# Row factors of attention pairs 3 to 15 sent as rows through memory, with idle products from the start and a new order of all steps

## The chip, the cores and the metric

The kernel runs on one core of one Trainium2 chip. The metric is device microseconds for one execution of the whole program: the lower the better. The core has five engines with a queue of instructions each: TensorE (PE in the profile, its weight loads PEld), VectorE (DVE), ScalarE (ACT), GpSimd (POOL) and SyncE (SP), which here only issues DMAs. Every engine takes its own instructions strictly in order and waits on semaphores that other engines or DMAs raise.

## The reference

32 graphs of 256 nodes with 128 features each pass four layers; each layer is added to its input and normalized over the features.

```python
# layers 0 and 1: graph attention
h = x @ W.T
z = (h @ a_src)[:, :, None] + (h @ a_dst)[:, None, :]
alpha = softmax(where(adj == 0, -big, leaky_relu(z, 0.2)))
x = layernorm(x + alpha @ h)
# layer 2: gated scores; adj is 0 or 1 here
alpha = sigmoid(where(adj == 1, leaky((x * a0) @ x.T), -big))
x = layernorm(x + alpha @ x + bias2)
# layer 3: relation 1 only
x = layernorm(x + (adj == 1) @ x @ W3[0] + bias3)
```

## The kernel before, in words

The graphs go in 16 pairs, n = 0 to 15 (H = 2 graphs a pair). A step, as `weight0:5`, is one stage of one layer for one pair; `ORDER` lists, for each of the five engines, the steps in the order in which that engine takes them, written out by hand. `counts` turns the lists into semaphore values, so that a step waits until the steps it reads from are done. `BANKS` says which of the eight 2 KB PSUM banks each PE step of each pair writes; `bank_free` makes PE wait until the former holder of the bank was read.

In an attention layer a pair passes these steps. PE projects (`h`, line 1097): besides the 128 features each node gets two logits, which VectorE copies out (`logits`, lines 811 and 813). Softmax of a leaky sum factors: apart from a factor that cancels in the normalization, the weight of node j for node i is the larger of a factor of i and a factor of j, times j's value factor, where the edge exists. ScalarE takes the exponentials of the logits (`gains`, line 609: 128 x 8). The factor of j is a column in SBUF, one number in each partition. The factor of i is wanted as a row, the same 256 numbers in all 128 partitions. `rows` (line 1114) makes it on PE: four transposes for a pair, each of a column of `gain` broadcast to 128 columns, into a PSUM bank. `weight` (line 837) is then four VectorE instructions for a pair: larger of row (from PSUM) and column, times the mask. PE multiplies the weights with the values (`out`, line 1157). Beside this path `dT` (line 1103) transposes the other logit into 4 rows for the largest (`peak`, `top`, `dmax`), from which the values' exponent is offset.

Layer 2 goes `xT`, `xTa`, `score` (line 1124), `sigmoid`, `umax`, `alpha`, `out2`; layer 3 `high`, `low`, `agg` (line 1134), `out3` (line 1154). Statistics (`stats`, line 888), residuals (`res`, lines 868 and 880) and small steps on VectorE, powers (`pow`, line 535), bias sums (`bias`, line 530), scaled copies (`xTa`, line 559), low parts (`low`, line 541) and some normalizations (line 549) on GpSimd stand between them.

GpSimd issues the mask loads, at most `AHEAD` = 6 pairs ahead of `weight0`. SP issues the loads of x, as rows (`x`) and turned (`xT`), and the stores. PE begins with five products of zeros (`idle_products`, line 1165) after the waits for the identity matrix, which GpSimd makes after its memset of `zero`.

Of the kernel before, what the change touches and what calls it, by code (L numbers as in the profile page):

```python
# [1287 lines left out]
```

## Time and profile before

| what | value |
|---|---|
| median of 3 runs (lowest to highest) | 253.18 us (252.33 to 253.56) |
| the profiled execution | 254.48 us |
| span of that execution | 251.4 us |
| PE busy | 227.2 us (90%) |
| VectorE busy | 229.2 us (91%) |
| ScalarE, GpSimd busy | 189.8 us (75%), 173.4 us (69%) |
| mean granted TensorE clock | 0.982 of full speed |

The profile is of one execution. The span runs from the first instruction of the program to the last; 3.1 us of the execution lie around it. Busy time is the time in which at least one instruction of an engine runs. Successive VectorE or PE instructions overlap by some tens of nanoseconds, so a mean duration of one is longer than the step from one to the next: 16 products of line 1157 take 1.79 us in the chain, 0.11 us each, where one lasts 0.277 us. A product of 32-bit numbers is two records in the trace, a transpose is one. The chain is followed back from the last instruction, at each step to what released it.

### The profile page before, as it was taken

Reading aid. Unit: us, or ns where it says so; the run is one execution under the profiler, and the core shown is the slowest. Engines: PE = TensorE matmul, PEld = TensorE weight load, DVE = VectorE, ACT = ScalarE, POOL = GpSimd, SP = SyncE. Lnnn points to the kernel's source line nnn. Section 1 sums busy time; section 2 is a strip of 40 time slices with the busy share of each in tenths; the row PEclk is TensorE's granted clock in tenths of the full one; section 3 lists DMA queues with packets and bytes.
Section 4 is the critical chain, followed back from the end, with each engine's and each line's share of the span. In section 5 each row is a group of like instructions: output and inputs, shape, how many; then the busy total and the mean of one; then the engine's idle time right before and its main releaser. Section 6 shows DMA issues by size and latency. Waiting matters only on the chain.

```text
span 251.4 us, 5755 instructions
## 1 busy us (share of the span) xinstructions
PE 227.2 (90%) x1745; PEld 206.6 (82%) x1745; DVE 229.2 (91%) x812; ACT 189.8 (75%) x587; POOL 173.4 (69%) x260
## 2 busy tenths in 40 slices
PE   4998899999999999999999998999999979897850
PEld 4896788987999998988898997989989968776840
DVE  0399989998999999999999999999999888999894
ACT  2497856988968998867998956996891966977752
POOL 6032049878756786789837529984797996699982
PEclk9999999999999999999999999999999979999995
DMA  6999124501452313212230300011000110100106
GB/s 180 252 262 240 52 83 86 126 4 42 83 127 39 88 18 94 104 20 68 54 116 10 117 1 33 14 42 44 1 0 3 42 44 1 43 0 3 42 1 214
DMA packets 12144, 17.56 MB, mean 70 GB/s; under 512 B 1104, under 2 KB 5968, under 8 KB 12112
## 3 DMA queue, kind: packets, MB, share of 16 engines
q1 hardware_dynamic: 9520, 12.85, 16.4%
q0 software_dynamic: 2304, 4.20, 9.9%
q8 instruction: 15, 0.25, 0.4%
q10 hardware_dynamic: 288, 0.14, 0.2%
q14 instruction: 17, 0.14, 0.2%
HBM read 17.17 MB, written 4.19 MB: 85 GB/s over the span
## 4 chain that ended last, share of the span: by engine, by line
PE 55%; DVE 33%; DMA 5%; issue 3%; ACT 2%; POOL 1%; DVEq 0%; SPq 0%; POOLq 0%
PE banks L1157 25%; PE banks L1097 8%; DVE wgt_all L837 7%; PE banks L1124 6%; DVE fstats L888 6%; DMA w<-in_L_gnn_weight 5%; PE banks L1082 4%; DVE fres_all L880 4%; DVE fres_all L868 3%; PE banks L1154 3%; DVE banks L802 3%; PE banks L1114 3%; DVE wgt_all L845 2%; PE banks L1134 2%; PE banks L1107 1%
## 5 line engine op out<-in xcount | busy, mean ns | idle before, releaser
L535 POOL TENSOR_TENSOR frstd<-fvar,minus_half 128x4 f32<-128x4 f32 x64 | 64.8, 1018 | 23.3 <-ACT fvar L674 15.5
L1157 PE MATMUL banks<-vals_all,wgt_all 128*128 128x129 f32 x512 | 63.5, 277 | 3.6 <-ACT vals_all L625 1.9
L1157 PEld LDWEIGHTS banks<-vals_all,wgt_all 128*128 128x128 f32 x512 | 59.6, 191 | 6.6 <-ACT vals_all L625 3.1
L837 DVE SCALAR_TENSOR_TENSOR wgt_all<-banks,gain,mask_all 128x256 f32<-128x256 f32 x128 | 52.6, 471 | 0.3 <-PE banks L1114 0.2
L530 POOL TENSOR_TENSOR xb_all<-xs_all,bias_cen 128x256 f32<-128x256 f32 x62 | 44.5, 737 | 9.5 <-ACT xs_all L668 4.4
L888 DVE BATCH_NORM_STATS2 fstats<-fres_all 128x6 f32<-128x256 f32 x128 | 47.5, 414 | 0.1
L668 ACT ACTIVATE xs_all<-fres_all,frstd 128x128 f32<-128x128 f32 x112 | 35.7, 409 | 0.7 <-POOL frstd L535 0.6
L1157 PE MATMUL banks<-xs_all,wgt_all 128*128 128x128 f32 x256 | 32.7, 283 | 2.6 <-DVE wgt_all L845 2.5
L1157 PEld LDWEIGHTS banks<-xs_all,wgt_all 128*128 128x128 f32 x256 | 30.7, 196 | 3.8 <-DVE wgt_all L845 3.7
L1124 PE MATMUL banks<-fxT,fxTa 128*128 128x256 f32 x128 | 30.3, 381 | 0.0
L605 ACT COPY fxT<-banks 128x256 f32<-128x256 f32 x64 | 20.3, 382 | 12.7 <-PE banks L1082 12.7
L1124 PEld LDWEIGHTS banks<-fxT,fxTa 128*128 128x128 f32 x128 | 23.1, 190 | 2.7
L868 DVE SCALAR_TENSOR_TENSOR fres_all<-banks,xb_all 128x512 f32<-128x512 f32 x32 | 21.5, 679 | 3.5 <-PE banks L1157 2.1
L1114 PE MATMUL banks<-ident,gain 128*128 128x128 f32 x128 | 19.7, 279 | 1.6 <-ACT gain L609 1.2
L802 DVE TENSOR_TENSOR banks<-banks,wgt_all 128x512 f32<-128x512 f32 x32 | 20.9, 687 | 0.3
L641 ACT ACTIVATE wgt_all<-banks 128x512 f32<-128x512 f32 x32 | 19.3, 603 | 2.3 <-PE banks L1124 2.1
L541 POOL TENSOR_TENSOR fxTa<-xs_all,fxTa 128x256 f16<-128x256 f32 x28 | 18.2, 671 | 3.6 <-ACT fxTa L648 3.6
L845 DVE SCALAR_TENSOR_TENSOR wgt_all<-banks,mask_all 128x512 f32<-128x512 f32 x32 | 20.4, 678 | 0.0
L1134 PE MATMUL banks<-mask_all,fxTa 128*128 128x256 bf16 x128 | 16.8, 273 | 3.6 <-POOL fxTa L541 2.1
L1097 PE MATMUL banks<-w_fast,xT_all 128*128 128x130 f32 x128 | 19.4, 299 | 0.5 <-DVE w_fast L740 0.3
L625 ACT ACTIVATE vals_all<-banks,fscale 128x128 f32<-128x128 f32 x64 | 18.1, 377 | 2.0 <-POOL fscale L570 1.1
L642 ACT ACTIVATE banks<-banks 128x512 f32<-128x512 f32 x32 | 19.5, 609 | 0.0
(93 smaller groups left out, 419.2 us busy)
## 6 DMA issues: line engine op xcount, KB each, us to landing
xT_all<-x_turned SPq DMA_DIRECT2D x16, 256.0 KB, 2.9
mask_all<-adj_turned POOLq DMA_DIRECT2D x16, 256.0 KB, 6.0
x_all<-x_laid SPq DMA_DIRECT2D x16, 256.0 KB, 2.8
out<-xs_all SPq DMA_DIRECT2D x16, 256.0 KB, 2.2
bias<-biases_laid SPq DMA_DIRECT2D x1, 128.0 KB, 12.0
w_pack<-W_and_columns ACTq DMA_DIRECT2D x1, 68.0 KB, 3.2
w_fast<-W_turned ACTq DMA_DIRECT2D x1, 64.0 KB, 3.6
w_nat<-in_L_gnn_W SPq DMA_DIRECT2D x1, 64.0 KB, 8.3
```

The costliest lines, as they stand in the source:

```text
L530: nc.gpsimd.tensor_tensor(xb(u)[:, :, :], xs(u)[:, :, :], bias_cen[:, int(l) - 2, :, :], ALU.add).then_inc(fast_pool[k], 1)
L535: nc.gpsimd.tensor_tensor(frstd[:, int(l), slot(n), :], fvar[:, int(l), slot(n), :], minus_half[:, :, :], ALU.pow).then_inc(fast_pool[k], 1)
L668: last = nc.scalar.activation(xs(u)[:, b, :], fres(u)[:, b, :], ACT.Copy, scale=frstd[:, int(l), u, b:b + 1])
L802: nc.vector.tensor_tensor(scored, scored, wgt(u), ALU.max).then_inc(fast_dve[k], 1)
L837: last = nc.vector.scalar_tensor_tensor(out=wgt(u)[:, c, :], in0=place(f"rows{l}", u), scalar=gain[:, u, c, 1:2], in1=maskT(u)[:, c, :], o ...
L845: nc.vector.scalar_tensor_tensor(out=wgt(u), in0=scored, scalar=1.0, in1=maskT(u), op0=ALU.add, op1=ALU.mult).then_inc(fast_dve[k], 1)
L868: nc.vector.scalar_tensor_tensor(out=fres_all[:, pair(n, FRES), :, :], in0=gathered, scalar={"2": 0.5, "3": 1.0}[l], in1=xb_all[:, pair(n, ...
L888: nc.vector.bn_stats(fstats[:, u, :, :].rearrange("p b k -> p (b k)"), fres(u)[:, :, :].rearrange("p b d -> p d b")).then_inc(fast_dve[k], 1)
L1097: last = nc.tensor.matmul(place(f"h{l}", u)[:, b * HC:(b + 1) * HC], (xT_in if l == "0" else fxT)(u)[:, b * P:(b + 1) * P], w_fast[:, int( ...
L1114: last = nc.tensor.transpose(place(f"rows{l}", u)[:, b * P:(b + 1) * P], gain[:, u, b, 0:1].to_broadcast([P, P]), ident[:, :])
L1124: last = nc.tensor.matmul(place("score", u)[:, c * N:(c + 1) * N], fxTa(u)[:, c * P:(c + 1) * P], fxT(u)[:, :], start=True, stop=True)
L1157: last = nc.tensor.matmul(place(f"out{l}", u)[:, b * width:(b + 1) * width], wgt(u)[:, c, b * P:(b + 1) * P], (vals if l in "01" else xs)( ...
```

## The change

Row factors of pairs 0 to 2 stay as they are, in both layers. For pairs 3 to 15:

- `dT` transposes both logits of the pair, into two PSUM banks, instead of one.
- ScalarE takes the exponential of the turned logit (`rowx`, 4 x 128 from PSUM, into a small tile in SBUF; two such tiles for each layer).
- SP sends the tile as one row of 512 numbers to memory (`rowa`, 2 KB) and, when that has landed, loads the row into all 128 partitions (`rows`, 256 KB; `ROWS` = 3 buffers for each layer).
- `weight` reads the row from SBUF, and waits for `gains` and for that load. The PE step `rows` is gone for these pairs.

Besides: `AHEAD` is 3. The first four loads of `x` wait for `h0` of their pair. VectorE makes `zero`; PE's waits for the identity stand behind the idle products, which are seven. At five places in its list PE gets `warm` steps: a wait for the bank of the step behind, and then 5, 11, 5, 3 and 10 products of zeros into it. All five lists and `BANKS` are written anew. Three bias sums and one low part more stand on VectorE, one normalization of layer 1 fewer.

```diff
-AHEAD = 6
+AHEAD = 3
+ROWS, ROW_OUT = 3, 2
...
-    "rows0": "4 5 3 7 2 3 1 1 7 0 3 1 3 1 4 5",
+    "rows0": "4 4 4 - - - - - - - - - - - - -",
...
+SPREAD = {l: [n for name, layer, n in order("sp") if name + layer == "rows" + l] for l in "01"}
...
+        rows_all = sb("rows_all", [P, 2, ROWS, H * N])
+        row_all = sb("row_all", [H * NB, 2, ROW_OUT, P])
...
             def load_x(l, n, k):
                 if n >= X_IN:
                     sp.wait_ge(fast_dve[(n - X_IN) % K], at("dve", "res0", final(n - X_IN)))
+                else:
+                    sp.wait_ge(fast_pe[n], at("pe", "h0", final(n)))
...
+            def send_row(l, n, k):
+                q = SPREAD[l].index(n)
+                sp.wait_ge(fast_act[k], at("act", f"rowx{l}", n * H))
+                sp.dma_start(row_scratch[int(l), n].rearrange("(a d) -> a d", d=P), row_tile(l, n)).then_inc(fast_row_out[int(l)][q % ROW_OUT], 16)
+
+            def spread_rows(l, n, k):
+                q = SPREAD[l].index(n)
+                sp.wait_ge(fast_row_out[int(l)][q % ROW_OUT], 16 * (q // ROW_OUT) + 16)
+                if q >= ROWS:
+                    m = SPREAD[l][q - ROWS]
+                    sp.wait_ge(fast_dve[m % K], at("dve", f"weight{l}", final(m)))
+                sp.dma_start(rows_all[:, int(l), q % ROWS, :], row_scratch[int(l), n].rearrange("(a d) -> a d", a=1).to_broadcast([P, H * N])).then_inc(fast_rows_in[int(l)][q % ROWS], 16)
...
-            nc.gpsimd.memset(zero[:, :], 0.0).then_inc(zero_set, 1)
...
+            def exponential_rows(l, n, k):
+                q = SPREAD[l].index(n)
+                act.wait_ge(fast_pe[k], at("pe", f"dT{l}", n * H))
+                if q >= ROW_OUT:
+                    act.wait_ge(fast_row_out[int(l)][q % ROW_OUT], 16 * (q // ROW_OUT))
+                nc.scalar.activation(row_tile(l, n), place(f"h{l}", final(n))[0:H * NB, 260:260 + P], ACT.Exp, scale=SLOPE - 1).then_inc(fast_act[k], 1)
...
+            nc.vector.memset(zero[:, :], 0.0).then_inc(zero_set, 1)
...
             def weights(l, n, k):
-                dve.wait_ge(fast_pe[k], at("pe", f"rows{l}", final(n)))
+                spread = n in SPREAD[l]
+                if spread:
+                    q = SPREAD[l].index(n)
+                    dve.wait_ge(fast_act[k], at("act", f"gains{l}", n * H))
+                    dve.wait_ge(fast_rows_in[int(l)][q % ROWS], 16 * (q // ROWS) + 16)
+                else:
+                    dve.wait_ge(fast_pe[k], at("pe", f"rows{l}", final(n)))
...
-                        last = nc.vector.scalar_tensor_tensor(out=wgt(u)[:, c, :], in0=place(f"rows{l}", u), scalar=gain[:, u, c, 1:2],
+                        last = nc.vector.scalar_tensor_tensor(out=wgt(u)[:, c, :], in0=rows_in(l, u) if spread else place(f"rows{l}", u), scalar=gain[:, u, c, 1:2],
                                                               in1=maskT(u)[:, c, :], op0=ALU.max, op1=ALU.mult)
...
-            pe.wait_ge(ident_set, 2)
-            pe.wait_ge(ident_bf_set, 2)
...
             def gather_d(l, n, k):
                 pe.wait_ge(fast_dve[k], at("dve", f"logits{l}", n * H))
+                if n in SPREAD[l]:
+                    nc.tensor.transpose(place(f"h{l}", final(n))[0:H * NB, 260:260 + P], logit[:, int(l), slot(n), :, 0].rearrange("p u b -> p (u b)"), ident[:, :])
...
+            def keep_warm(count, phase, u):
+                bank_free(phase, u)
+                idle_products(count, bank_of(phase, u))
...
-            idle_products(5)
+            idle_products(7, 5)
             projection_columns()
-            for step, l, n in order("pe"):
-                steps[step](l, n, n % K)
+            pe.wait_ge(ident_set, 2)
+            pe.wait_ge(ident_bf_set, 2)
+            sequence = order("pe")
+            for q, (step, l, n) in enumerate(sequence):
+                if step == "warm":
+                    following, layer, m = sequence[q + 1]
+                    keep_warm(n, following + layer, m * H)
+                else:
+                    steps[step](l, n, n % K)
```

Where the lists move instructions is shown at three places, as the instructions stand in an engine's queue: line, operation, what is written and read, columns, count.

The beginning of PE's queue. Before, behind the waits for the identity: zeros, the product that gives the logits' columns, the projections of pairs 0 and 1, and then for each of these its logits' turn (`banks<-ident,logit`) and rows (`banks<-ident,gain`).

```order
L1165 MATMUL banks<-zero 128x128 x5
L1037 MATMUL banks<-w_pack 128x2
L1097 MATMUL banks<-w_fast,xT_all 128x130 x8
L1103 MATMUL banks<-ident,logit 4x128
L1114 MATMUL banks<-ident,gain 128x128 x4
L1103 MATMUL banks<-ident,logit 4x128
L1107 MATMUL banks<-ident,top 128x4 x2
L1114 MATMUL banks<-ident,gain 128x128 x4
L1157 MATMUL banks<-vals_all,wgt_all 128x129 x16
```

The same place now.

```order
L1210 MATMUL banks<-zero 128x128 x7
L1080 MATMUL banks<-w_pack 128x2
L1140 MATMUL banks<-w_fast,xT_all 128x130 x8
L1148 MATMUL banks<-ident,logit 4x128
L1159 MATMUL banks<-ident,gain 128x128 x4
L1086 MATMUL banks<-ident,w_cen 128x128
L1087 MATMUL banks<-w_pack,w_cen 128x2
L1148 MATMUL banks<-ident,logit 4x128
L1152 MATMUL banks<-ident,top 128x4
L1140 MATMUL banks<-w_fast,xT_all 128x130 x4
```

The turn of the second projection (`w_cen`) has come forward to between the rows of pairs 0 and 1, and the projection of pair 2 follows where the rows of pair 1 and the first outputs stood.

The middle of PE's queue, around pair 12 of layer 0 before: its logits' turn, an output of layer 1 for pair 9, its largest, its rows, an output of layer 2.

```order
L1103 MATMUL banks<-ident,logit 4x128
L1157 MATMUL banks<-vals_all,wgt_all 128x129 x8
L1107 MATMUL banks<-ident,top 128x4
L1114 MATMUL banks<-ident,gain 128x128 x4
L1157 MATMUL banks<-xs_all,wgt_all 128x128 x8
```

The same pair now; the rows in front are pair 13's two logit turns and a `warm` step.

```order
L1147 MATMUL banks<-ident,logit 4x128
L1148 MATMUL banks<-ident,logit 4x128
L1210 MATMUL banks<-zero 128x128 x5
L1125 MATMUL banks<-ident,xs_all 128x128 x4
L1202 MATMUL banks<-vals_all,wgt_all 128x129 x8
L1147 MATMUL banks<-ident,logit 4x128
L1148 MATMUL banks<-ident,logit 4x128
L1202 MATMUL banks<-vals_all,wgt_all 128x129 x8
L1152 MATMUL banks<-ident,top 128x4 x2
```

For the same pair the second transpose of the logits has come (line 1147), and the four transposes of `gain` behind the output are gone; the largest of pairs 12 and 13 stand together.

VectorE's queue ahead of the weights of layer 1, pair 3. Before: steps of layer 2 for pairs 0 and 1 (`res2`, statistics), logits and largest of other pairs, and then the weights of pair 6 (layer 0) and pair 3.

```order
L823 TENSOR_REDUCE minus_dmax<-banks 128x1
L845 SCALAR_TENSOR_TENSOR wgt_all<-banks,mask_all 128x512 x2
L868 SCALAR_TENSOR_TENSOR fres_all<-banks,xb_all 128x512
L813 TENSOR_TENSOR logit<-banks,frstd 128x4 x2
L888 BN_STATS fstats<-fres_all 128x6 x2
L868 SCALAR_TENSOR_TENSOR fres_all<-banks,xb_all 128x512
L819 TENSOR_REDUCE top<-banks 4x1
L888 BN_STATS fstats<-fres_all 128x6 x2
L811 COPY logit<-banks 128x4 x2
L823 TENSOR_REDUCE minus_dmax<-banks 128x1
L819 TENSOR_REDUCE top<-banks 4x1
L837 SCALAR_TENSOR_TENSOR wgt_all<-banks,gain,mask_all 128x256 x8
```

The same pair now. Its logits stand eight rows further up than the first row here; in between are one residual step (4 instructions) and one pair of statistics.

```order
L940 SCALAR_TENSOR_TENSOR fvar<-fstats,fvar 128x4
L851 COPY logit<-banks 128x4 x2
L859 TENSOR_REDUCE top<-banks 4x1
L853 TENSOR_TENSOR logit<-banks,frstd 128x4 x2
L859 TENSOR_REDUCE top<-banks 4x1
L863 TENSOR_REDUCE minus_dmax<-banks 128x1 x2
L859 TENSOR_REDUCE top<-banks 4x1
L948 SCALAR_TENSOR_TENSOR fcenter<-fstats,frstd 128x4
L863 TENSOR_REDUCE minus_dmax<-banks 128x1
L867 TENSOR_TENSOR fscale<-vals_all,frstd 128x4
L863 TENSOR_REDUCE minus_dmax<-banks 128x1
L883 SCALAR_TENSOR_TENSOR wgt_all<-rows_all,gain,mask_all 128x256 x4
```

The large operations of layer 2 are no longer between the logits and the weights of this pair, and the weights read `rows_all`, and so wait for the load, where they read a PSUM bank.

## Rows read from the trace of the kernel before

**Rows 1.** The windows: busy time of each engine in each stretch (first row: columns).
```profile
core 0: us, PE busy (x) PEld busy (x) DVE busy (x) ACT busy (x) POOL busy (x), PEclk, DMA share, GB/s
...
0.00:12.00 12.00, 8.46 (x40) 7.75 (x40) 2.40 (x14) 3.75 (x8) 4.28 (x13) 1.00 0.86 213
...
40.00:200.00 160.00, 156.88 (x1246) 144.65 (x1245) 156.57 (x557) 130.02 (x413) 119.67 (x176) 1.00 0.21 52
200.00:210.00 10.00, 8.19 (x52) 7.49 (x52) 7.60 (x26) 5.58 (x19) 7.61 (x12) 0.83 0.09 32
...
240.00:251.40 11.40, 2.35 (x18) 1.79 (x18) 7.25 (x24) 4.24 (x15) 6.47 (x8) 0.76 0.36 119
```

**Rows 2.** The chain that ended last, in 40 to 200 us, shares by line.
```profile
by line: PE banks L1157 32.8%; DVE wgt_all L837 10.1%; PE banks L1124 9.9%; PE banks L1097 8.9%; PE banks L1082 5.9%; PE banks L1114 4.5%; DVE fstats L888 3.8%; DVE fres_all L880 3.7%; PE banks L1154 3.6%; PE banks L1134 2.7%; issue 2.3%; P
```

**Rows 3.** The same chain in order of time: start, duration in us, what.
```profile
35.93 0.44 PE banks L1114 x4
```

**Rows 4.** Groups by line: count, busy us, mean ns of one, idle before.
```profile
L837 DVE SCALAR_TENSOR_TENSOR wgt_all<-banks,gain,mask_all 128x256 f32<-128x256 f32 x128 | 52.6, 471 | 0.3 <-PE banks L1114 0.2
...
L888 DVE BATCH_NORM_STATS2 fstats<-fres_all 128x6 f32<-128x256 f32 x128 | 47.5, 414 | 0.1
...
L541 POOL TENSOR_TENSOR fxTa<-xs_all,fxTa 128x256 f16<-128x256 f32 x28 | 18.2, 671 | 3.6 <-ACT fxTa L648 3.6
...
L625 ACT ACTIVATE vals_all<-banks,fscale 128x128 f32<-128x128 f32 x64 | 18.1, 377 | 2.0 <-POOL fscale L570 1.1 <-DVE fscale L827 0.8
...
L902 DVE SCALAR_TENSOR_TENSOR fcenter<-fstats,frstd 128x4 f32<-128x4 f32 x16 | 3.7, 231 | 0.0
...
L775 DVE TENSOR_TENSOR fxTa<-xs_all,fxTa 128x256 f16<-128x256 f32 x4 | 1.8, 476 | 0.0
...
L769 DVE TENSOR_TENSOR xb_all<-xs_all,bias_cen 128x256 f32<-128x256 f32 x2 | 0.7, 418 | 0.0
```

**Rows 5.** Timeline of PE, 2.8 to 18.5 us: start, duration, operation, idle before.
```profile
2.91 2.47 PE L1165 MATMUL banks<-zero 128*128 128x128 f32 x10 [2.91 <-DVE ones_col L723]
...
5.91 3.84 PE L1097 MATMUL banks<-w_fast,xT_all 128*128 128x130 f32 x16 [0.32 <-DVE w_fast L740]
...
17.29 1.06 PE L1097 MATMUL banks<-w_fast,xT_all 128*128 128x130 f32 x8
```

**Rows 6.** Timeline of VectorE, 112.5 to 117 us.
```profile
113.03 0.16 DVE L894 SCALAR_TENSOR_TENSOR fvar<-fstats,fvar 128x4 f32<-128x4 f32 x1
...
114.68 0.62 DVE L827 TENSOR_TENSOR fscale<-vals_all,frstd 128x4 f32<-128x4 f32 x1
...
115.36 0.62 DVE L902 SCALAR_TENSOR_TENSOR fcenter<-fstats,frstd 128x4 f32<-128x4 f32 x1
```

**Rows 7.** Timeline of GpSimd over the same time.
```profile
111.72 1.83 POOL L559 TENSOR_SCALAR fxTa<-fxT,w_pack 128x256 f32<-128x256 f32 x2 [0.39 <-PE banks L1114]
...
114.56 1.40 POOL L530 TENSOR_TENSOR xb_all<-xs_all,bias_cen 128x256 f32<-128x256 f32 x2
```

**Rows 8.** Line 902 by itself: count, shortest, median and longest duration in ns.
```profile
L902 DVE SCALAR_TENSOR_TENSOR fcenter<-fstats,frstd x16: 118/154/627, 36.6 to 222.3; 128x4 f32<-128x4 f32 x16
```

**Rows 9.** Line 530 of GpSimd in the same view.
```profile
L530 POOL TENSOR_TENSOR xb_all<-xs_all,bias_cen x62: 713/727/1302, 38.9 to 240.4; 128x256 f32<-128x256 f32 x62
```

**Rows 10.** DMA issues by line: count, KB each, median us to landing.
```profile
xT_all<-x_turned SPq DMA_DIRECT2D x16, 256.0 KB, 2.9
mask_all<-adj_turned POOLq DMA_DIRECT2D x16, 256.0 KB, 6.0
...
out<-xs_all SPq DMA_DIRECT2D x16, 256.0 KB, 2.2
```

**Rows 11.** The windows, 204 to 208 us; columns as in rows 1.
```profile
204.00:206.00 2.00, 1.90 (x12) 1.93 (x13) 2.00 (x5) 0.99 (x4) 2.00 (x4) 0.72 0.15 50
206.00:208.00 2.00, 2.00 (x12) 2.00 (x10) 0.99 (x3) 0.00 (x0) 2.00 (x4) 0.50 0.03 8
```

**Rows 12.** Timeline of PE, 202 to 208 us.
```profile
204.10 3.04 PE L1157 MATMUL banks<-xs_all,wgt_all 128*128 128x128 f32 x16 [0.64 <-DVE wgt_all L845]
```

More of the change, by code:

```diff
@@ L161 @@
 BANKS = {
[13 rows of a table removed]
[13 rows of a table added]
 }
-WHOLE = tuple(n + l for n in ("dT", "top", "gains", "v", "logits", "peak", "dmax", "rsum", "rinv", "var", "center", "pow") for l in "0123") + ("fscale", "seen", "res2", "res3")
+WHOLE = tuple(n + l for n in ("dT", "top", "gains", "rowx", "v", "logits", "peak", "dmax", "rsum", "rinv", "var", "center", "pow") for l in "0123") + ("fscale", "seen", "res2", "res3")
 PHASES = {"turn": 1, "h0": H, "rows0": 1, "out0": H, "xT1": 1, "h1": H, "rows1": 1, "out1": H,
@@ L216 @@
 UP_SQUARE = UP * UP
-COUNTS = {"pe": counts("pe", apart=("turn",)), "act": counts("act"), "dve": counts("dve", apart=("centre", "judge")), "pool": counts("pool", apart=("mask",))}
+COUNTS = {"pe": counts("pe", apart=("turn", "warm")), "act": counts("act"), "dve": counts("dve", apart=("centre", "judge")), "pool": counts("pool", apart=("mask",))}
 def at(engine, name, u):
@@ L255, with res_gnn_kernel @@
 HELD_BEFORE = holders()
-def res_gnn_kernel(nc, x, adj, W0, a_src0, a_dst0, W1, a1, a2_0, a2_1, a2_2, a2_3, bias2, adj3, W3, bias3, x_laid, x_turned, adj_turned, W0_turned, W0_and_columns, biases_laid, out):
+SPREAD = {l: [n for name, layer, n in order("sp") if name + layer == "rows" + l] for l in "01"}
+def res_gnn_kernel(nc, x, adj, W0, a_src0, a_dst0, W1, a1, a2_0, a2_1, a2_2, a2_3, bias2, adj3, W3, bias3, x_laid, x_turned, adj_turned, W0_turned, W0_and_columns, biases_laid, row_scratch, out):
     B, N, D = x.shape
@@ L333, in res_gnn_kernel @@
         wgt_all = sb("wgt_all", [P, WGT * H, NB, N])
-        sg_all = sb("sg_all", [P, SG * H, NB, N])
+        rows_all = sb("rows_all", [P, 2, ROWS, H * N])
+        row_all = sb("row_all", [H * NB, 2, ROW_OUT, P])
+        sg_all = rows_all[:, :, :, :].rearrange("p l q n -> p (l q n)")[:, 0:SG * H * NB * N].rearrange("p (q b n) -> p q b n", b=NB, n=N)
         logit = sb("logit", [P, 2, B, NB, 2])
@@ L373, in wgt, with rows_in, row_tile @@
             return wgt_all[:, u % (WGT * H), :, :]
+        def rows_in(l, u):
+            q = SPREAD[l].index(u // H) % ROWS
+            return rows_all[:, int(l), q, u % H * N:(u % H + 1) * N]
+        def row_tile(l, n):
+            return row_all[:, int(l), SPREAD[l].index(n) % ROW_OUT, :]
         def hi(u):
@@ L420, in res_gnn_kernel @@
         fast_pool = [sem(f"fast_pool_{k}") for k in range(K)]
+        fast_row_out = [[sem(f"fast_row_out_{l}{q}") for q in range(ROW_OUT)] for l in range(2)]
+        fast_rows_in = [[sem(f"fast_rows_in_{l}{q}") for q in range(ROWS)] for l in range(2)]
         fast_stored = [sem(f"fast_stored_{q}") for q in range(XS)]
@@ L477, in load_weights @@
                 sp.dma_start(dst, src).then_inc(signal, 16)
-            steps = {"weights": load_weights, "x": load_x, "xT": load_xT, "store": store}
+            steps = {"weights": load_weights, "x": load_x, "xT": load_xT, "rowa": send_row, "rows": spread_rows, "store": store}
             for step, l, n in order("sp"):
@@ L674, in variances @@
                 nc.scalar.activation(fvar[:, int(l), slot(n), :], fstats[:, slot(n), :, 2], ACT.Copy, bias=floor, scale=factor).then_inc(fast_act[k], 1)
-            steps = {"seen": note_odd, "var": variances, "xT": copy_xT, "gains": gains, "v": exponentials, "vals": values, "xTa": copy_xTa, "sigmoid": sigmoids,
+            steps = {"seen": note_odd, "var": variances, "xT": copy_xT, "gains": gains, "rowx": exponential_rows, "v": exponentials, "vals": values, "xTa": copy_xTa, "sigmoid": sigmoids,
                      "high": high_part, "agg": copy_gathered, "norm": normalize}
@@ L1162, in _, with idle_products @@
                      "score": scores, "agg": gather, "out": outputs, "turn": projection_turn}
-            def idle_products(count):
+            def idle_products(count, taken):
                 for _ in range(count):
-                    nc.tensor.matmul(banks[:, 5, 0:P], zero[:, :], zero[:, :], start=True, stop=True)
+                    nc.tensor.matmul(banks[:, taken, 0:P], zero[:, :], zero[:, :], start=True, stop=True)
+            def keep_warm(count, phase, u):
+                bank_free(phase, u)
+                idle_products(count, bank_of(phase, u))
             pe.wait_ge(zero_set, 1)
-            idle_products(5)
+            idle_products(7, 5)
             projection_columns()
-            for step, l, n in order("pe"):
-                steps[step](l, n, n % K)
+            pe.wait_ge(ident_set, 2)
[7 more added lines that the diff above has]
+                    steps[step](l, n, n % K)
             for n in range(TEAMS - K, TEAMS):
@@ L1283 @@
         args.append(nc.dram_tensor(name, a.shape, mybir.dt.from_np(a.dtype), kind="ExternalInput").ap())
+    args.append(nc.dram_tensor("row_scratch", (2, T, H * N), F32, kind="Internal").ap())
     args.append(nc.dram_tensor("out", (B, P, NB, D), F32, kind="ExternalOutput").ap())
```

197 rows, old and new, of tables (BANKS, ORDER) are left out of this document.

## The prediction

> **What bounds the kernel now.** I read the windows first, then the chain, then the groups by line, then timelines at the start, at a place where VectorE meets GpSimd, and at the tail. The windows show two engines at their limit at once: from 40 to 200 us PE is busy 156.88 of 160 us and VectorE 156.57 [rows 1]. Outside that stretch VectorE has its slack: 2.40 busy of the first 12 us, 7.60 of 200 to 210, 7.25 of the last 11.4. The chain of 40 to 200 us changes hands between both; PE's `rows` transposes (line 1114) are 4.5% of it, 7.2 us, and VectorE's weights (line 837) 10.1%, 16.2 us [rows 2]. The reader should see that a PE instruction taken away is worth at most what VectorE can follow: in that stretch VectorE waits only 160 - 156.57 = 3.4 us.
>
> The sum is made against the profiled execution, 254.48 us: span 251.4 and 3.1 around it. It is 1.3 above the median, 253.18; that is taken off at the end.
>
> **PE.** For 13 pairs in two layers four transposes go: 13 x 2 x 4 = 104. Four take 0.44 us, 0.11 each [rows 3]: 11.4 us. One transpose for each of the 26 comes, at the same 0.11: 2.9. The five `warm` steps hold 5 + 11 + 5 + 3 + 10 = 34 products of two records each, 68 x 0.11 = 7.5 us. They cost nothing where PE would wait for its next input anyway, and up to 7.5 where it would not. So PE loses between 8.5 and 1.0 us of work. Against VectorE's 3.4 us of waiting I take half: **-1.7**; ends 0 and -3.4.
>
> **VectorE.** 104 weights instructions read their row from SBUF instead of PSUM; the trace has none such. With a PSUM row one takes 471 ns [rows 4]. The nearest with 256 columns and two SBUF inputs are the bias sum, 418, and the low part, 476; with one SBUF input the statistics take 414 [rows 4]. The ends are 104 x -57 = -5.9 and 104 x +5 = +0.5. I take the bias sum, also 32 bit to 32 bit: 104 x -53 = -5.5. To VectorE come six bias instructions (6 x 0.42) and two low parts (2 x 0.48); four normalizations go, which I put at a bias sum each, and three small products come at 0.15 [rows 4, 8]: 2.5 + 1.0 - 1.7 + 0.5 = +2.3.
>
> Then the price of two SBUF inputs. At 114.68 and 115.36 us two VectorE instructions of four columns last 0.62 each [rows 6], while GpSimd is in its bias sums, 1.40 us for two [rows 7]. Both read two SBUF tensors. Line 902 alone lasts 154 in the median and 627 at the longest, mean 231 [rows 4, 8]: 77 ns lost for each instruction. At 113.03 a like instruction lasts 0.16 although GpSimd is in a scaled copy (line 559) [rows 6, 7]. So what holds VectorE up is GpSimd's instructions with two large inputs (lines 530 and 541), not all of its work. The weights now become such instructions. They come in 26 bursts of four; if only the first of a burst is exposed, 26 x 77 ns = 2.0 us, if each is, 104 x 77 ns = 8.0. GpSimd also yields: its line 530 has lasted 1302 instead of 727 [rows 9], which says that VectorE, once in, can keep going. I take +3.0, near the lower end for that reason. VectorE in sum: -5.5 + 2.3 + 3.0 = **-0.2**; ends -1.6 with 2.0 and -5.9, and +10.8 with 8.0 and +0.5.
>
> The page "SBUF — State Buffer" of the Trainium skill (section "Who interferes with whom") says that a VectorE instruction with two SBUF inputs contends with any GpSimd instruction that reads SBUF, and that the later one waits for the whole of the other. For the sums of lines 530 and 541 the trace agrees; for line 559 it does not [rows 6, 7]. By the page as it stands the loss would be larger than my +3.0; that is the second rival.
>
> **The way through memory.** From the logits to the weights a spread pair now needs: two transposes on PE with their lag, 0.4; the exponential, 128 columns from PSUM, like a value step 0.38 [rows 4]; the row to memory; the row back. The trace has neither DMA. The nearest to memory is a store, 2.2 us for 256 KB, the nearest back a load, 2.9 [rows 10]. The path is 0.4 + 0.38 + 2.2 + 2.9 = 5.9 us, without time in the queues of PE, ScalarE and SP; with 6.0 for the last DMA, as the masks have it [rows 10], it is 9.0. What covers it is VectorE's own work between logits and weights. I counted it in the new queue. For layer 1, pair 3 stand four residual instructions and two statistics (0.33 each, their 0.41 less the overlap) and some 22 small ones at about 0.08: 3.7 us. For pair 4 it is 4.7, for the other 24 at least 6.4, for 20 of them at least 7.0. So two are late for certain, by 2.2 and 1.2; behind the waiting weights stand all of VectorE's later steps, and PE's outputs wait for them. Part falls on waits that are there anyway: **+2.0**, ends 0 and +10.7 (a path of 7.5, which makes ten pairs late).
>
> SP is in order: while it waits for a row to land, loads of x and stores stand behind. Their data are wanted some steps later; nothing is counted. `AHEAD` = 3 lets a mask go only when the weights three pairs back are done; a mask lands in 6.0 in the median [rows 10], and between `weight0` of pairs three apart stands about that much of VectorE's work or more; nothing is counted either, and both are in the upper end.
>
> **The start.** PE's first product of zeros runs at 2.91, having waited for the identity [rows 5]. Now it waits for VectorE's memset alone, some 2 us earlier; two more products of 2 x 0.25 us each eat 1.0 of that. The projections of pairs 0 and 1 take 3.84 for 16 records, 0.24 each, and later 1.06 for 8 [rows 5]: the slow rate is the lower of PE's two clock levels as the steps show it, though the granted clock is 1.00 there. If PE is at its fast rate as much earlier as it begins, half of the 16 gain 0.11 each, 0.9. The column product, which all of it waits for, moves by at most 0.6. I take **-1.3**; ends 0 and -2.5.
>
> **The tail.** From 204 to 208 us the granted clock is 0.72 and then 0.50 [rows 11], after PE had been mostly waiting (8.19 busy of 200 to 210, [rows 1]). Sixteen products take 3.04 us [rows 12], where at 0.11 they take 1.8, and VectorE waits 2.4 us in those ten. A `warm` step of ten products now stands in this part of the program. I take 1.2 of clock and a third of the waits: **-2.0**; ends 0 and -3.6.
>
> **Sum.** -1.7 - 0.2 + 2.0 - 1.3 - 2.0 = -3.2: 254.48 - 3.2 = 251.3, less 1.3 for the median: 250.0.
>
> **Rivals.**
> 1. *PE is the bound and VectorE follows.* For: the chain is on PE for most of 40 to 200. Against: VectorE has 3.4 us to give. It would give the chain's 7.2, less half of the new transposes (1.4), 16.2 x 53/471 = 1.8 of the weights, 1.3 and 2.0 at the ends: -10.9, 242.3 us.
> 2. *The shared way into SBUF turns the weights slow* (slower). Place: every weights instruction while GpSimd is in lines 530 or 541. Those are 62 x 0.727 = 45.1 and 18.2 us [rows 4, 9], a quarter of the span; met there, an instruction waits half of 0.72. All 104 exposed: 104 x 0.25 x 0.36 = 9.4 in place of 3.0, +6.4, 256.4 us. It decides from a loss of about 6.2, where the sum is zero. If all of GpSimd's work held VectorE (119.67 of 160 us, [rows 1]), it would be 104 x 0.75 x 0.36 = 28 us, +25. Against: the undisturbed case above.
> 3. *The rows land late* (slower): a path of 7.5 makes ten pairs wait, 10.7 in place of 2.0: 258.7 us. For: three in-order queues lie on the path, and a load can stand behind another. Against: most gaps hold over 7 us.
> 4. *Nothing is gained in the middle or the tail*: VectorE sheds nothing, its waits only move. -1.3 - 0.2 + 2.0 = +0.5: 253.7 us. That the rows do leave PE, but to no effect, is this case.
>
> **How the numbers follow.** Forecast 0.45, with a range of its own from 246.5 to 252; rivals 0.10, 0.15, 0.15, 0.15. What a measurement here can tell from no change is about 0.5%, 1.27 us: faster is under 251.9, slower over 254.5. Faster: 0.42 of the forecast, all 0.10 of the first rival, 0.03 of the fourth: 0.55. Same: 0.02 of the forecast, 0.11 of the fourth, 0.04 of the second and third: 0.17. Slower: 0.28. The range that leaves out two in ten reaches from 243.5, by the first rival, to 257, between the second and the third.
>
> **What the profile would show.** Right: the weights at 0.42 with a few at 1.0; the first projection before 5.5 us; VectorE's waits for DMA only at two or three weights; 40 to 200 with PE busy some 6 us less and VectorE as before. Wrong: a mean of the weights over 0.50 (second rival), VectorE waiting for `rows_all` by more than 5 us (third), PE still busy 156 in that stretch with products of zeros, or VectorE's waits grown as PE's work fell.

## The result: slower by 7.5%, and the profile after

The changed kernel takes 271.81 us in the median of five (271.5 to 278.88), the kernel before 253.45 in the same set (252.33 to 253.6): a ratio of 1.0745 (95% interval 1.0714 to 1.0775, as in every bracket behind a ratio below), +18.4 us. A second set gave 1.0835 (1.0763 to 1.0906). The forecast was 250.0, faster; its range ended at 257. The rows of after come from a later profiled execution (span 270.8 us) whose time lies with the median; the first one took 278.88.

The windows, with the columns of [rows 1]:

```profile
0.00:12.00 12.00, 10.30 (x52) 9.81 (x53) 3.99 (x21) 5.52 (x10) 2.50 (x10) 1.00 0.89 234
12.00:40.00 28.00, 22.38 (x180) 19.66 (x179) 25.14 (x113) 18.12 (x62) 7.22 (x13) 1.00 0.67 169
40.00:200.00 160.00, 144.21 (x1110) 132.40 (x1109) 147.89 (x506) 120.30 (x385) 114.62 (x154) 0.97 0.31 84
200.00:210.00 10.00, 8.82 (x66) 7.57 (x64) 9.93 (x37) 8.39 (x29) 8.86 (x11) 1.00 0.25 81
```

In 40 to 200 us PE was busy 156.88 of 160 us and is now busy 144.21; VectorE went from 156.57 to 147.89. Both bounds have become loose at once: each waits 9 to 13 us more there, for the other engines. Then the groups by line that answer to [rows 4, 9], with GpSimd's small ones:

```profile
L883 DVE SCALAR_TENSOR_TENSOR wgt_all<-rows_all,gain,mask_all 128x256 f32<-128x256 f32 x104 | 48.2, 523 | 2.7 <-ACT vals_all L664 1.2 <-issue 0.9 <-DMA rows_all<-row_scratch 0.4
...
L567 POOL TENSOR_TENSOR frstd<-fvar,minus_half 128x4 f32<-128x4 f32 x64 | 67.5, 1061 | 13.4 <-DVE fvar L940 7.5 <-ACT fvar L713 3.3 <-DVE fvar L944 0.7
L562 POOL TENSOR_TENSOR xb_all<-xs_all,bias_cen 128x256 f32<-128x256 f32 x56 | 42.0, 768 | 12.8 <-ACT xs_all L704 8.0 <-ACT xs_all L707 4.7
...
L581 POOL TENSOR_SCALAR xs_all<-fres_all,frstd,fcenter 128x128 f32<-128x128 f32 x28 | 15.9, 578 | 1.2 <-DVE fcenter L948 1.1
...
L597 POOL TENSOR_SCALAR fvar<-fstats 128x4 f32<-128x4 f32 x25 | 8.3, 332 | 16.8 <-DVE fstats L934 16.4
```

The same views of single lines (shortest, median and longest ns, then first and last start):

```profile
L597 POOL TENSOR_SCALAR fvar<-fstats x25: 184/195/1934, 22.4 to 255.7; 128x4 f32<-128x4 f32 x25
...
L567 POOL TENSOR_TENSOR frstd<-fvar,minus_half x64: 996/1017/2614, 22.7 to 265.4; 128x4 f32<-128x4 f32 x64
...
L883 DVE SCALAR_TENSOR_TENSOR wgt_all<-rows_all,gain,mask_all x104: 456/477/1020, 25.9 to 233.4; 128x256 f32<-128x256 f32 x104
```

The weights are at 523 ns in the mean, above the 500 that the prediction named as the sign of its second rival. The surprise is on GpSimd: a variance of four columns that takes 0.195 us in the median lasts up to 1.934, a power of 1.017 up to 2.614. In before their longest were 0.37 and 1.08 us:

```profile
L565 POOL TENSOR_SCALAR fvar<-fstats x24: 193/197/367, 17.3 to 241.1; 128x4 f32<-128x4 f32 x24
...
L535 POOL TENSOR_TENSOR frstd<-fvar,minus_half x64: 997/1014/1078, 17.6 to 246.1; 128x4 f32<-128x4 f32 x64
```

Where that happens the timelines say why. VectorE, 82 to 97 us (start, duration, operation, idle before):

```profile
82.82 1.65 DVE L883 SCALAR_TENSOR_TENSOR wgt_all<-rows_all,gain,mask_all 128x256 f32<-128x256 f32 x4
84.41 0.27 DVE L859 TENSOR_REDUCE top<-banks 4x1 f32<-4x128 f32 x1
84.61 1.65 DVE L883 SCALAR_TENSOR_TENSOR wgt_all<-rows_all,gain,mask_all 128x256 f32<-128x256 f32 x4
86.19 0.21 DVE L863 TENSOR_REDUCE minus_dmax<-banks 128x1 f32<-128x4 f32 x2
87.19 0.16 DVE L948 SCALAR_TENSOR_TENSOR fcenter<-fstats,frstd 128x4 f32<-128x4 f32 x1 [0.79 <-POOL frstd L567]
...
89.73 3.49 DVE L883 SCALAR_TENSOR_TENSOR wgt_all<-rows_all,gain,mask_all 128x256 f32<-128x256 f32 x4
...
96.71 0.69 DVE L914 SCALAR_TENSOR_TENSOR fres_all<-banks,xb_all 128x512 f32<-128x512 f32 x1 [3.49 <-PE banks L1202]
```

GpSimd at the same time:

```profile
82.64 1.93 POOL L597 TENSOR_SCALAR fvar<-fstats 128x4 f32<-128x4 f32 x1
84.54 2.61 POOL L567 TENSOR_TENSOR frstd<-fvar,minus_half 128x4 f32<-128x4 f32 x1
...
89.72 1.59 POOL L562 TENSOR_TENSOR xb_all<-xs_all,bias_cen 128x256 f32<-128x256 f32 x2 [0.32 <-ACT xs_all L707]
91.28 1.66 POOL L573 TENSOR_TENSOR fxTa<-xs_all,fxTa 128x256 f16<-128x256 f32 x2
```

The variance ends when the first burst of four weights does, 84.57 against 84.47; the power behind it then loses the whole second burst, 2.61 - 1.02 = 1.6 us. VectorE itself waits 0.79 us for that power, and ScalarE's normalization 2.21. Five microseconds later it is the other way round: GpSimd's bias sums and low parts are under way, and four weights take 3.49 us instead of 1.65.

PE over the same time:

```profile
84.61 0.40 PE L1152 MATMUL banks<-ident,top 4*128 4x4 f32 x3
89.28 5.06 PE L1210 MATMUL banks<-zero 128*128 128x128 f32 x22 [4.27 <-DVE wgt_all L891]
94.13 2.14 PE L1202 MATMUL banks<-xs_all,wgt_all 128*128 128x128 f32 x13
```

PE waits 4.27 us for the gated weights (line 891), which have fallen behind, and only then do the products of zeros run, 5.06 us of them, ahead of outputs that need the same weights and could have started at 89.28. VectorE then waits 3.49 us, its longest wait of the whole run, for outputs that stand behind these zeros (its row at 96.71). The granted clock is already down by then:

```profile
88.00:90.00 2.00, 0.72 (x3) 0.73 (x4) 2.00 (x5) 1.13 (x4) 1.68 (x3) 0.60 0.77 129
90.00:92.00 2.00, 2.00 (x12) 2.00 (x10) 2.00 (x3) 1.97 (x8) 2.00 (x3) 0.50 0.81 133
```

### The profile page after: what moved, and what is told of

Its sections match the earlier page's. It is cut to its first block and busy times, and to the rows that moved or that the text cites. A ratio compares the mean times of both kernels' runs of the same rounds, so it can differ in the third digit from the quotient of the medians.

```text
span 277.1 us, 5858 instructions
## 1 busy us (share of the span) xinstructions
PE 237.2 (86%) x1739; PEld 214.6 (77%) x1739; DVE 238.4 (86%) x819; ACT 197.4 (71%) x617; POOL 180.4 (65%) x249
## 5 line engine op out<-in xcount | busy, mean ns | idle before, releaser
L567 POOL TENSOR_TENSOR frstd<-fvar,minus_half 128x4 f32<-128x4 f32 x64 | 67.7, 1064 | 14.7 <-DVE fvar L940 8.9
L1202 PE MATMUL banks<-vals_all,wgt_all 128*128 128x129 f32 x512 | 66.1, 284 | 4.0 <-DVE wgt_all L883 1.9
L1202 PEld LDWEIGHTS banks<-vals_all,wgt_all 128*128 128x128 f32 x512 | 63.2, 200 | 5.3 <-ACT vals_all L664 2.2
L883 DVE SCALAR_TENSOR_TENSOR wgt_all<-rows_all,gain,mask_all 128x256 f32<-128x256 f32 x104 | 48.9, 530 | 3.3 <-DMA rows_all<-row_scratch 3.3
L562 POOL TENSOR_TENSOR xb_all<-xs_all,bias_cen 128x256 f32<-128x256 f32 x56 | 41.3, 757 | 12.8 <-ACT xs_all L704 8.0
L546 POOL DMA_DIRECT2D mask_all<-adj_turned x16 | 9.6, 602 | 35.9 <-DVE wgt_all L883 26.7
L1210 PE MATMUL banks<-zero 128*128 128x128 f32 x82 | 15.6, 365 | 12.2 <-DVE wgt_all L891 8.3
L1210 PEld LDWEIGHTS banks<-zero 128*128 128x128 f32 x82 | 14.2, 268 | 13.4 <-DVE wgt_all L891 9.2
L842 DVE TENSOR_TENSOR banks<-banks,wgt_all 128x512 f32<-128x512 f32 x32 | 21.1, 692 | 3.5 <-ACT banks L681 3.5
L654 ACT ACTIVATE vals_all<-logit,minus_dmax 128x4 f32<-128x4 f32 x32 | 9.6, 301 | 16.6 <-DVE minus_dmax L863 12.3
L629 ACT ACTIVATE odd_square<-mask_all,minus_half 128x1024 bf16<-128x1024 bf16 x16 | 18.4, 1151 | 3.8 <-DMA mask_all<-adj_turned 3.7
```

What stands on the lines that cost most here:

```text
L562: nc.gpsimd.tensor_tensor(xb(u)[:, :, :], xs(u)[:, :, :], bias_cen[:, int(l) - 2, :, :], ALU.add).then_inc(fast_pool[k], 1)
L567: nc.gpsimd.tensor_tensor(frstd[:, int(l), slot(n), :], fvar[:, int(l), slot(n), :], minus_half[:, :, :], ALU.pow).then_inc(fast_pool[k], 1)
L842: nc.vector.tensor_tensor(scored, scored, wgt(u), ALU.max).then_inc(fast_dve[k], 1)
L883: last = nc.vector.scalar_tensor_tensor(out=wgt(u)[:, c, :], in0=rows_in(l, u) if spread else place(f"rows{l}", u), scalar=gain[:, u, c, 1:2],
L1202: last = nc.tensor.matmul(place(f"out{l}", u)[:, b * width:(b + 1) * width], wgt(u)[:, c, b * P:(b + 1) * P], (vals if l in "01" else xs)( ...
L1210: nc.tensor.matmul(banks[:, taken, 0:P], zero[:, :], zero[:, :], start=True, stop=True)
```

## The experiments

Three theories: A, weights with both inputs in SBUF and GpSimd hold each other up; B, something of the way through memory (late rows, SP's queue, `AHEAD`); C, the new order by itself, with the steps of zeros as its special case. Ratios are against runs of before in the same set.

**a0_again, a6_after.** The changed kernel unaltered.

> The changed kernel once more, for a second profile. Expected by every theory: 271.5 to 272.6 us, granted clock 0.97 to 0.98, and VectorE and PE both idle some 15 us more than before, in small pieces all over 12 to 120 us and 200 us to the end. If VectorE's idle time sits instead in one or two long waits, the theory that the new order as a whole is looser falls at once.

> The changed kernel itself, timed beside the next three on one chip. Expected by every theory: 271 to 276 us, 1.07 to 1.09 of before.

276.0 us in one run, above the 272.6 that was expected, and 272.82 in the median of four. The idle time lies in many pieces; PE's largest, 4.27 us, and VectorE's, 3.49, are in the place shown above.

**a1_ahead6.** `AHEAD = 3` -> `AHEAD = 6`.

> The changed kernel with AHEAD = 6 as before, nothing else. Theory that GpSimd's queue is held up (its mask steps wait 26.7 us for the weights three pairs back, and its sums and powers stand behind them): 5 to 12 us back, 260 to 267 us. Theory that the new order as a whole is looser, or that rows come late, or that the shared way into SBUF slows VectorE: within 2 us of 271.8.

275.51 us, 1.0836 (1.0753 to 1.0919): no time back. The 24 us that GpSimd's mask steps wait for weights in the changed kernel are not what costs: here these waits are gone, and GpSimd's variances wait for VectorE's statistics instead, 33.6 us in sum where it was 16.4.

**a2_nowarm, d4_nowarm.** In PE's list:

```
- "... out1:3 warm:5 out1:1 xT2:0 ..."    + "... out1:3 out1:1 xT2:0 ..."    (and the other four)
```

> The changed kernel without the five steps of zeros (34 products) in the middle of PE's order; the seven at the start stay. Theory that these steps, which wait for a bank in PE's in-order queue, hold up what stands behind them: 4 to 8 us back, 264 to 268 us, with PE's waits for the banks gone. Theory that they only fill waits that the next step has anyway: within 2 us of 271.8. If they really keep the clock up, slower by 1 to 4 us and a lower granted clock.

> The changed kernel without the steps of zeros in the middle, a second time, on the chip of d1 to d3. As before: 1.054 to 1.072 of before, 266 to 271 us.

1.0629 (1.0543 to 1.0715) and 1.0666 (1.0591 to 1.0741): 2 to 5 us back against the changed kernel's 1.0745 and 1.0835; against the first of these two the intervals overlap. The wait that stood ahead of the zeros now stands ahead of the outputs, and as long. PE's waits in the changed kernel, then without the steps of zeros:

```profile
PE banks L1210 <- DVE wgt_all L891: 8.6, 4, 4.3
PE banks L1210 <- ACT vals_all L664: 2.9, 1, 2.9
```

```profile
PE banks L1202 <- DVE wgt_all L891: 7.7, 4, 4.4
PE banks L1125 <- ACT vals_all L664: 3.1, 2, 2.9
```

(us in total, times, longest.) The zeros filled none of it.

**a3_rows_ready.** No row goes out to memory, and the broadcast reads what is there:

```
- sp.wait_ge(fast_row_out[...], ...);  sp.dma_start(rows_all[...], row_scratch[int(l), n]...)
+ sp.dma_start(rows_all[...], x_laid[n, 0]...)
```

(Cut; the `rowa` steps and ScalarE's wait for them go too.)

> The changed kernel with rows that need no trip: the broadcast into all partitions reads 512 numbers of x, which lie in memory from the start, and no row goes out to memory; SP no longer waits for ScalarE's exponentials nor for a row to land. Left out: the true row factors (the exponentials are still computed). Size and number of the broadcasts stay. Theory that the rows land late and that SP's queue is held up by them: 8 to 16 us back, 256 to 264 us. Theory that the new order or the shared way into SBUF costs the time: within 4 us of 271.8 (VectorE's direct waits for rows are only 3.3 us).

269.61 us, 1.0631 (1.054 to 1.0723): 3 to 5 us back, not the 8 to 16 that B asked for; against the first set the intervals overlap here too. Late rows are at most a part, not the cause.

**a4_one_input.** The weights as `tensor_scalar(wgt, rows_all[..., ::2], gain, 1.0, max, mult)`.

> The changed kernel, but the weights of pairs 3 to 15 read one SBUF tensor instead of two: max of the row and the gain, every second number of the two rows of the pair. Left out: the mask. Rows, waits, orders and DMAs stay. Theory that the weights with both inputs in SBUF and GpSimd hold each other up (in the changed kernel's second profile GpSimd's instructions last 14 us longer in sum than at their median, in pieces of up to 1.7 us, and 63 weights last 549 ns against 475): 10 to 18 us back, 254 to 262 us, GpSimd's variances and powers at 0.2 and 1.0 us throughout. Theory that the new order is looser by itself: within 4 us of the changed kernel (272 to 276), plus what a shorter weights instruction gives VectorE.

260.48 us in one run and 265.5 to 265.78 in three: too scattered for a ratio. It points to A but does not isolate it: the new instruction is shorter (0.346 us), and it too lasted 0.406 in the mean of the 64 that met GpSimd, whose variances still reached 1.09 us. A stand-in had to be found that does not meet GpSimd; c1 has it.

**b1_port.** In before, the operand alone, with a wait for the constant that it now reads, which is set once near the start:

```
+ if n >= 3: dve.wait_ge(bias_cen_set, 4)
- in0=place(f"rows{l}", u)
+ in0=bias_cen[:, 0, :, :].rearrange("p b d -> p (b d)") if n >= 3 else place(f"rows{l}", u)
```

> The kernel before, in its own order with its transposes on PE, but the weights of pairs 3 to 15 read their row from a constant SBUF tensor (the centred bias) instead of PSUM. Left out: the row factor's values. Nothing else moves. Theory that weights and GpSimd hold each other up: 8 to 18 us slower than before, 261 to 271 us, with GpSimd's small instructions at up to 2 us. Theory that the new order or the way through memory costs the time: within 2 us of before (251 to 256).

267.56 us, 1.0598 (1.0553 to 1.0642): +14.5 us from one operand. Its groups:

```profile
L839 DVE SCALAR_TENSOR_TENSOR wgt_all<-bias_cen,gain,mask_all 128x256 f32<-128x256 f32 x104 | 53.2, 572 | 0.4 <-PE banks L1116 0.4
...
L559 POOL TENSOR_SCALAR fxTa<-fxT,w_pack 128x256 f32<-128x256 f32 x20 | 19.4, 976 | 0.9 <-ACT fxT L605 0.5
```

Against 471 ns in [rows 4] that is 104 x 101 = 10.5 us on VectorE, which bounds this kernel. One place in its timelines, VectorE and then GpSimd:

```profile
60.25 5.56 DVE L839 SCALAR_TENSOR_TENSOR wgt_all<-bias_cen,gain,mask_all 128x256 f32<-128x256 f32 x8
```

```profile
60.55 1.50 POOL L541 TENSOR_TENSOR fxTa<-xs_all,fxTa 128x256 f16<-128x256 f32 x2
...
63.72 1.41 POOL L530 TENSOR_TENSOR xb_all<-xs_all,bias_cen 128x256 f32<-128x256 f32 x2
```

Eight weights take 5.56 us; two undisturbed bursts take 3.3. A is shown, alone and in the old order. GpSimd's part is smaller here: its instructions last 8.3 us longer in sum than at their medians, and its variances and powers reach 0.49 and 1.55 us, not the 2 that was expected. Who held the weights also differs: nine that met only a scaled copy (line 559) lasted 575 ns in the mean.

**b2_early.** In before: VectorE's memset of `zero`, seven products and the column product ahead of the waits for the identity.

> The kernel before with the change's start alone: VectorE sets the zeros to zero, PE multiplies seven of them and makes the column product before it waits for the identity. If the start gives what was forecast: 1.3 us less, 252.0 us, ends 0 and -2.5. If the first projections are at the slow clock in some executions whatever stands ahead (2.02 us against 3.81 for 16 records in two profiles of the same start): no change in the median, within 0.5 us.

1.0017 (0.9986 to 1.0048). Nothing, though PE's start moved as forecast. Its PE timeline, then that of the changed kernel:

```profile
1.06 3.36 PE L1162 MATMUL banks<-zero 128*128 128x128 f32 x14 [1.06 <-DVE zero L720]
...
5.12 2.02 PE L1094 MATMUL banks<-w_fast,xT_all 128*128 128x130 f32 x16 [0.48 <-DVE w_fast L740]
```

```profile
1.06 3.36 PE L1210 MATMUL banks<-zero 128*128 128x128 f32 x14 [1.06 <-DVE zero L760]
4.21 0.43 PE L1080 MATMUL banks<-w_pack 128*128 128x2 f32 x2
5.12 3.81 PE L1140 MATMUL banks<-w_fast,xT_all 128*128 128x130 f32 x16 [0.48 <-issue]
```

The same start leads in one execution to projections at 0.13 us a record, in another to 0.24, as in [rows 5].

**b3_old_order.** Rows through memory, with the steps in the order of before.

> The rows of pairs 3 to 15 through memory in the order of before: the same steps as before on every engine, without the 104 transposes, with the exponential of the rows right behind the logits' transposes and the two DMAs where they are ready; AHEAD = 6, no steps of zeros in the middle. Four pairs have under 3 us from logits to weights there. Theory that weights and GpSimd hold each other up: 262 to 275 us (port 8 to 18, late rows some 5 more, less PE's 8). Theory that the new order is what costs: 250 to 260 us, since rows are late only at four pairs.

290.02 us, 1.1429 (1.1371 to 1.1488), above what either theory said. With the rows sent this way the old order is no remedy: it is 20 us slower than the changed kernel without its zeros (a2, 1.0629), which has them as little as b3 has. Where b3 loses the rest was not followed up; whether the new order by itself costs anything is read from d1 below.

**c1_stats, c2_stats_nowarm, c3_before_stats.** A stand-in of one SBUF input for 88 weights, in the changed kernel, in it without the zeros, and in before:

```
+ if n >= (7 if l == "0" else 3):
+     last = nc.vector.bn_stats(out=unused[:, int(l), u, c, :], in_=maskT(u)[:, c, :]); continue
```

> The changed kernel, but 88 of its 104 weights instructions (layer 0 from pair 7, layer 1 from pair 3) are statistics over the mask: 256 columns, one SBUF input, a form that lasts 414 ns beside GpSimd and 418 without it in the trace of before. Left out: these weights. All waits, rows and orders stay. The kernel of c3 carries the same statistics in before, so c1 is read against c3. Theory that weights with two SBUF inputs and GpSimd holding each other up is the whole cause: c1 within 3 us of c3, both 245 to 251 us, and GpSimd's variances at 0.20 us throughout. Theory that something else of the change costs too (the steps of zeros, rows that land late, the order): c1 4 to 8 us above c3. Theory that the two inputs are not the cause: c1 over 264 us.

> As c1, and without the five steps of zeros in the middle of PE's order. If these steps hold up what stands behind them in PE's queue, as the changed kernel without them said (268.2 against 272 to 276): 3 to 7 us below c1. If they matter only while GpSimd is held up: within 1 us of c1. If they do keep the clock: above c1.

> The kernel before with the same 88 statistics over the mask in place of its weights; PE still makes the rows. Left out: these weights. VectorE saves 88 x 0.06 = 5 us: 248 to 251 us by every theory, 253 if PE is the bound.

c1 1.0363 (1.0286 to 1.0441), c2 1.007 (1.0041 to 1.0099), c3 0.9918 (0.9889 to 0.9947). The 16 weights with two SBUF inputs that are left in c1 lost nothing, 473 ns in the mean. GpSimd is free again in c1:

```profile
L568 POOL TENSOR_TENSOR frstd<-fvar,minus_half 128x4 f32<-128x4 f32 x64 | 65.0, 1022 | 14.9 <-DVE fvar L944 7.5 <-ACT fvar L714 4.8 <-DVE fvar L948 0.7
L582 POOL TENSOR_SCALAR xs_all<-fres_all,frstd,fcenter 128x128 f32<-128x128 f32 x28 | 12.3, 450 | 1.5 <-DVE fcenter L952 1.3
L598 POOL TENSOR_SCALAR fvar<-fstats 128x4 f32<-128x4 f32 x25 | 4.9, 197 | 15.8 <-DVE fstats L938 15.5
```

"Two inputs are the whole cause" falls with c1, 11 us above c3, more than the 4 to 8 that was expected of the rest. The zeros cost 7.4 us (c1 to c2) in this kernel.

**d1_stats_ready, d2_nowarm_ready, d3_before_warm.** What was still open.

> As c2 (statistics in place of 88 weights, no steps of zeros in the middle), and the rows need no trip: the broadcast reads 512 numbers of x, and no row goes out to memory. Left out: 88 weights and the true row factors. c2 stood 4 us above c3. If late rows are those 4 us: 250 to 252 us, 0.99 of before, as c3. If the order itself costs them: as c2, 254 to 256. If the order gains what the forecast gave PE, the start and the tail: 246 to 248.

> The changed kernel without the steps of zeros in the middle and with rows that need no trip; weights with both inputs in SBUF. Left out: the true row factors. What stays of the loss should be that of the two inputs. If that is worth the 14.5 us of b1: 264 to 268 us. If it is only what lies between c1 and the changed kernel, 8 us: 257 to 261.

> The kernel before with the five steps of zeros alone (34 products), each ahead of the step that it stands ahead of in the changed kernel (out1 of pair 1, out2 of pairs 3 and 8, xT2 of pairs 8 and 11). In the changed kernel they begin after the bank has come free and take 11.3 us in sum. If they cost their PE time where PE is near its bound: 4 to 11 us slower, 257 to 264. If PE has the room (3 us idle in 40 to 200): under 3 us.

d1 0.9955 (0.9907 to 1.0003), d2 1.0531 (1.0486 to 1.0575), d3 1.0302 (1.0234 to 1.037). In d3 the zeros run for 8.5 us in sum without a wait ahead of them and cost 7.6 us; PE is busy as before, 156.82 of 160, and VectorE falls from 156.57 to 151.18:

```profile
40.00:200.00 160.00, 156.82 (x1257) 145.26 (x1256) 151.18 (x531) 125.33 (x396) 114.35 (x166) 1.00 0.20 51
```

Set side by side (yes: the cost is in):

| kernel | two SBUF inputs | zeros in the middle | rows by memory | ratio |
|---|---|---|---|---|
| changed | yes | yes | yes | 1.0745, 1.0835 |
| a3 | yes | yes | ready | 1.0631 |
| a2, d4 | yes | no | yes | 1.0629, 1.0666 |
| d2 | yes | no | ready | 1.0531 |
| c1 | no (stand-in) | yes | yes | 1.0363 |
| c2 | no (stand-in) | no | yes | 1.0070 |
| d1 | no (stand-in) | no | ready | 0.9955 |
| c3, before | no (stand-in) | no | by PE | 0.9918 |
| b1, before | yes | no | by PE | 1.0598 |
| d3, before | no (row in PSUM) | yes | by PE | 1.0302 |

Two inputs: d1 to d2, 0.0576 or 14.6 us; 2.1 of it (c3) is VectorE's gain by the stand-in, so about 12.5. Late rows: c2 to d1 2.9 us, d4 to d2 3.4. Zeros: 7.4 without the two inputs (c1 to c2), 2.5 beside them (a3 to d2, intervals that overlap; 2 to 5 by a2 and d4). That PE has more time to lose beside them is a likely reason, not a tested one. Together that is 12.5 + 3.4 and 2 to 5, some 18 to 21 us, and the two sets measured 18.4 and 21.1. What is left of the change, the transposes gone, the order and the start, is d1 against c3: +0.9 us, with intervals that overlap.

## Why the prediction was wrong

**The step that failed: "Then the price of two SBUF inputs", +3.0.** The two inputs cost 14.5 us alone (b1) and about 12.5 in the changed kernel. The prediction named the mechanism and, for its order, the partners: weights that met lines 562 and 573 (530 and 541 in before) lasted 0.75 to 0.91 us in the mean, those that met powers 0.47. Its rows 6 and 7 show a bias sum only, so that the low parts hold VectorE too was a guess that came true. Three things were wrong in it.
- It charged VectorE alone and put GpSimd's loss at nothing. In the changed kernel VectorE's weights themselves lost 104 x (523 - 477) = 4.8 us, inside the ends of 2.0 and 8.0. But a GpSimd instruction can be held too, and for a whole burst of four: lines 562, 567, 573, 581, 597 and 602 together last some 14 us longer than at their medians, and they feed the centres, the normalizations and the outputs. The prediction had the evidence in [rows 9], one bias sum at 1302 instead of 727 ns, and read it as relief for VectorE.
- It took the lower end of 2.0 to 8.0. In before's order VectorE alone lost 10.5. The second rival had the place, and the price passed the 6.2 from which it said it decides, so its chance of 0.15 was too small. But its 9.4 us charged VectorE alone as well; that it lies nearer to 12.5 is partly luck.
- It ruled out line 559 by one VectorE instruction of four columns. In b1 nine weights that met this line alone lasted 575 ns in the mean. In the changed kernel only two weights met it (line 591 there), 469 and 480 ns, so the error cost the forecast little.

The page "SBUF — State Buffer" of the Trainium skill (section "SBUF: two separate sides") says that of a VectorE instruction with two SBUF inputs and a GpSimd instruction that reads SBUF the one that starts first holds the shared ports for its whole length and the other blocks. The variance of 1.934 us agrees that the other blocks, and adds that a burst of instructions back to back counts as one. Which came first it does not show: its recorded start, 82.64, is ahead of the burst's, 82.82, and yet it was the one held.

**"PE", the steps of zeros, at most 7.5 us and free where PE waits.** Wrong in kind. A `warm` step waits for the bank of the step behind it, which that step would have waited for itself: without the zeros the same waits stand at the outputs and transposes, as long as before (a2). So the zeros begin when the work could. They take 1.38 + 5.06 + 1.38 + 0.94 + 2.50 = 11.3 us, at 0.22 a record at 90 us where the clock is granted at 0.50. Nor did they hold the clock at the longest of these waits: it is at 0.50, the lower level, before they begin at 89.28.

**"VectorE", weights from SBUF, -5.5.** Nothing was gained. Where no GpSimd instruction meets them they last 478 ns in the mean, with the row in PSUM 471 [rows 4]. The bias sum's 418, from which 53 ns were taken, was the wrong neighbour: another operation, with another second input.

**"The way through memory", +2.0.** Near in size, 2.9 to 3.4 us, but not by the two pairs that it named. From the exponential's start to the landing of the row it took 4.4 us at least, 5.8 in the median and 10.0 at most; 5.9 was forecast from the logits. Five rows landed within 0.1 us ahead of their weights: pairs 3, 4 and 6 of layer 0 and pairs 3 and 8 of layer 1. Of the two that were named, pairs 3 and 4 of layer 1, only the first is among them; the early ones flew 3.9 to 5.5 us beside other loads.

**"The start", -1.3, and "the tail", -2.0.** The first projection starts at 5.12, under 5.5 as said, but b2 shows that it gives nothing. For the tail the prediction read "mostly waiting" from 8.19 of 10 us busy, which says the opposite; the wait is in 202 to 204, with PE busy 0.62 of 2.00 us. In 200 to 210 us the clock stays at 1.00 in place of 0.83, and without the zeros (a2) it is at 0.83 again. But of the six profiles with the zeros in this order two have a fall near there all the same (at 218.6 us in the first of the changed kernel, at 208.4 in c1), so whether the zeros hold the clock there stays open. The 2.50 us of zeros at 212.54, behind 2.89 of waiting, are more than the 1.2 that the clock was to give back. No run has the tail's step alone; d1 and c3 have no zeros in the middle.

**The bound.** "A PE instruction taken away is worth at most what VectorE can follow" is borne out as far as it was tried: with the three costs out, d1, the 104 transposes fewer are worth nothing that can be measured. Of the signs for the wrong side two came as written: weights over 0.50, and VectorE's waits grown as PE's work fell. Of those for the right side the first projection (5.12) and VectorE's few waits for rows came too, though the forecast was wrong.

## What to carry to other kernels

Before an operand moves from PSUM into SBUF, count the VectorE instructions that then read two SBUF tensors, and price both sides: what VectorE loses behind GpSimd, and what every GpSimd instruction loses behind a VectorE burst, with all that waits for it. Products meant to keep PE busy must wait for something that is free earlier than what the next real step needs, or they add to the wait. And where two engines are both at their limit, do not count on a change that relieves one: here 104 transposes fewer on PE gave nothing measurable.

## What the runs showed of the hardware

- A short GpSimd instruction is held for a whole burst of VectorE's: 0.195 us became 1.934 beside four weights of 1.65.
- GpSimd's powers (four columns, 1.02 us) do not hold the weights (473 ns for the 20 that met only them) though a power too was held (2.614 us in place of 1.017); its bias sums and low parts over 256 columns do (751 and 891 ns in the mean for the five and three that met only these), and in b1 its scaled copies too (575 for nine).
- `tensor_scalar` from SBUF to SBUF with a single tensor input meets GpSimd as well (0.406 us against 0.346 in a4); the statistics, also of one input, do not (0.406 where they met GpSimd in c1, 0.410 where they did not).
- The same instructions at the start give PE's first 16 projections in 2.02 or in 3.81 us, from one execution to the next.
